# The normaliser of a gated linear-attention block: absolute value moved to ScalarE, EPS folded in once per group

## The reference, cut to what matters

```python
log_f = jax.nn.log_sigmoid(fg)
cs = jnp.cumsum(log_f, axis=1)
log_D = where(tril, cs[:, :, None] - cs[:, None, :], -inf) + ig[:, None, :]
max_log_D = jnp.max(log_D, axis=-1, keepdims=True)
D_mat = jnp.exp(log_D - max_log_D)
C = (qk / sqrt(DH)) * D_mat
normalizer = jnp.maximum(jnp.abs(C.sum(axis=-1, keepdims=True)), jnp.exp(-max_log_D))
h = jnp.einsum('hst,htd->hsd', C / (normalizer + EPS), vh)       # EPS = 1e-6
h = layernorm(h) * ln_scale
...
x = x + tanh(g_xattn) * h_all_heads
h = jnp.square(jax.nn.relu(layernorm(x) @ W_fc.T)); y = h @ W_proj.T
x = x + tanh(g_ffn) * mean(five spike steps of y)
```

## Time and profile before

| | |
|---|---|
| three runs | 617.12, 615.51 and 617.72 us, median 617.12 us |
| profiled execution, span from first to last instruction | 615.3 us; the page gives no other time for it |
| instructions | 17747 |
| busy: PE, DVE, ACT, POOL | 571.4, 526.3, 485.8, 493.3 us |
| share of the chain that ended last: PE | 82% |
| the same: queue of SP, DMA | 7%, 3% |

### The profile page before, as it was taken

How to read it: one execution, slowest core, us unless ns; L and a number is a source line. 1 busy time by engine, 2 the same in 40 slices (tenths; PEclk the granted TensorE clock), 3 DMA queues, 4 the chain that set the end, 5 groups by cost and what they waited for, 6 DMA issues and landing times.

```text
span 615.3 us, 17747 instructions
## 1 busy us (share of the span) xinstructions
PE 571.4 (93%) x6032; PEld 479.2 (78%) x6032; DVE 526.3 (86%) x1291; ACT 485.8 (79%) x1011; POOL 493.3 (80%) x541
## 2 busy tenths in 40 slices
PE   0568988999999999999999999999999999999995
PEld 0357888887888888888788888888888888887894
DVE  4789889989989898989989898989999888878446
ACT  3776878897888888888888788888888777776673
POOL 4878889996997889887997889887997887955542
PEclk9995989999999999999999999999999999999998
DMA  8775736664664637662663637752675427401002
GB/s 271 168 145 115 160 74 124 168 139 95 124 149 96 155 84 127 171 146 70 123 163 83 158 83 131 187 126 70 121 167 130 87 48 148 121 4 35 0 2 70
DMA packets 73193, 71.34 MB, mean 116 GB/s; under 512 B 8720, under 2 KB 68752, under 8 KB 73104
## 3 DMA queue, kind: packets, MB, share of 16 engines
q1 hardware_dynamic: 71888, 70.00, 50.5%
q10 hardware_dynamic: 1216, 0.21, 0.2%
HBM read 27.44 MB, written 8.39 MB: 58 GB/s over the span
## 4 chain that ended last, share of the span: by engine, by line
PE 82%; SPq 7%; DMA 3%; ACT 2%; issue 2%; DVE 2%; POOL 1%; ACTq 0%; POOLq 0%; DVEq 0%
PE z_ps L1069 28%; PE y_ps L1135 26%; PE qk_ps L773 4%; PE arg_ps L758 4%; PE misc_ps L503 4%; SPq L706 3%; PE misc_ps L569 2%; SPq L553 2%; PE pv_ps L822 2%; PE pv_ps L820 2%; PE pv_ps L821 2%; PE pv_ps L897 2%; DMA x<-w_proj_t 2%; PE y_ps L1164 1%; PE arg_ps L1135 1%
## 5 line engine op out<-in xcount | busy, mean ns | idle before, releaser
L802 POOL TENSOR_TENSOR c_lo<-decay 128x512 bf16<-128x512 f32 x128 | 132.7, 1043 | 31.9 <-DVE decay L792 31.8
L1112 POOL TENSOR_TENSOR sq_lo<-w_raw,sq_hi 128x512 fp32r<-128x512 f32 (+1 forms) x96 | 111.8, 1166 | 39.6 <-ACT w_raw L1092 39.3
L1069 PE MATMUL z_ps<-x_hi,wfc_hi 128*128 128x512 f32 (+1 forms) x288 | 114.4, 397 | 1.8 <-ACT w_raw L1079 1.8
L1069 PE MATMUL z_ps<-x_hi,wfc_lo 128*128 128x512 f32 (+1 forms) x288 | 106.1, 368 | 0.0
L1069 PE MATMUL z_ps<-x_lo,wfc_hi 128*128 128x512 f32 (+1 forms) x288 | 105.9, 368 | 0.0
L1135 PE MATMUL y_ps<-sq_hi,wpr_hi 128*128 128x512 f32 (+1 forms) x256 | 103.8, 406 | 0.0
L1135 PE MATMUL y_ps<-sq_hi,wpr_lo 128*128 128x512 f32 (+1 forms) x256 | 97.4, 380 | 0.0
L1135 PE MATMUL y_ps<-sq_lo,wpr_hi 128*128 128x512 f32 (+1 forms) x256 | 97.1, 379 | 0.0
L792 DVE TENSOR_TENSOR decay<-qk_ps,decay 128x512 f32<-128x512 f32 x128 | 87.0, 680 | 9.4 <-ACT decay L784 6.5
L784 ACT ACTIVATE decay<-arg_ps,lqk_col 128x512 f32<-128x512 f32 x128 | 86.6, 677 | 10.5 <-PE arg_ps L761 9.5
L1153 DVE SCALAR_TENSOR_TENSOR spikes<-y_ps,spikes 128x1024 bf16<-128x1024 f32 (+1 forms) x64 | 73.8, 1153 | 1.2
(11 more groups left out here) (193 smaller groups left out, 1727.8 us busy)
## 6 DMA issues: line engine op xcount, KB each, us to landing
x_in<-x SPq DMA_DIRECT2D x32, 256.0 KB, 3.2
kT_in<-ctx_cols SPq DMA_DIRECT2D x32, 256.0 KB, 3.2
v_in<-ctx_rows SPq DMA_DIRECT2D x32, 256.0 KB, 4.3
k_stack<-kT_hi SPq DMA_DIRECT2D x64, 128.0 KB, 3.2
k_stack<-kT_lo SPq DMA_DIRECT2D x64, 128.0 KB, 3.7
q_stack<-qT_hi SPq DMA_DIRECT2D x64, 128.0 KB, 4.1
q_stack<-qT_lo SPq DMA_DIRECT2D x64, 128.0 KB, 4.3
out<-w_raw SPq DMA_DIRECT2D x32, 256.0 KB, 3.4
```

The source lines that it names most:

```text
L802: e.tensor_tensor(c_lo[i % NCH][:, :], c, top(c), ALU.subtract).then_inc(sem("c_lo"), 1)
L1069: ins = e.matmul(z_ps[:, tokens(q)], lhsT, rhs, start=(n == 0), stop=(n == len(terms) - 1))
L1112: e.tensor_tensor(sq_lo[n % NSQ][:, tokens(q)], relu[n % NRE][:, tokens(q)], sq_hi[n % NSQ][:, tokens(q)].bitcast(fp32), ALU.subtract).the ...
```

## The change

`h_norm` is cut into six steps. On VectorE remain `h_scale` (the former L912), `h_add` (L913), `h_denom` (one scalar_tensor_tensor: add EPS, then max with the bound), `h_recip` (L918) and `h_norm` (L919); they stand next to each other at every place where `h_norm` stood. `h_abs` is new on ScalarE: Abs of the row sums, from PSUM to PSUM, once for each batch, 32 in all. `floor_eps` is new on GpSimd: it adds EPS to the bound, once for each of the ten groups, in place, ahead of `k_weigh` of the group's first batch. The tile `most` goes. Links within VectorE become semaphores of their own, waited for ahead of each step. The rest of the diff writes out loops that were there before (the order of the shared PSUM bank, and the programs' loops), with the same steps in the same order; TensorE's and SP's programs hold the same steps as before.

```diff
-        most = sb("most", [P, ST, NH], fp32)
...
+        def floor_eps(e, g):
+            if not 0 <= g < NG:
+                return
+            e.wait_ge(sem("fT_free"), g + 1)
+            least = floor[g % 3][:, 0:ST, 0:group_rows(g)]
+            e.tensor_scalar(least, least, EPS, None, ALU.add).then_inc(sem("floor_eps"), 1)
...
-            link(e, "vector", e.tensor_tensor(by_head(state_f[:, :]), inter_ps.rearrange("p c (g e) -> p c g e", g=HPC), since, ALU.mult))
-            link(e, "vector", e.tensor_tensor(pv_heads[:, 1, :, :], pv_heads[:, 1, :, :], late, ALU.add))
-            row_sum, least = pv_heads[:, :, :, DH], floor[g % 3][:, 0:ST, row:row + NH]
-            link(e, "vector", e.scalar_tensor_tensor(most[:, :, :], row_sum, -1.0, least, ALU.mult, ALU.max))
-            link(e, "vector", e.tensor_tensor(denom, row_sum, most[:, :, :], ALU.max))
-            link(e, "vector", e.tensor_scalar(denom, denom, EPS, None, ALU.add))
-            link(e, "vector", e.reciprocal(rdenom[:, :, :], denom))
+            e.tensor_tensor(by_head(state_f[:, :]), inter_ps.rearrange("p c (g e) -> p c g e", g=HPC), since,
+                            ALU.mult).then_inc(sem("h_scale"), 1)
+
+        def h_add(e, b):
+            e.wait_ge(sem("h_scale"), b + 1)
+            e.tensor_tensor(pv_heads[:, 1, :, :], pv_heads[:, 1, :, :], late, ALU.add).then_inc(sem("h_add"), 1)
+
+        def h_abs(e, b):
+            e.wait_ge(sem("h_add"), b + 1)
+            e.activation(denom, pv_heads[:, :, :, DH], ACT.Abs).then_inc(sem("h_abs"), 1)
+
+        def h_denom(e, b):
+            e.wait_ge(sem("h_abs"), b + 1)
+            if b == GROUPS[g][0]:
+                e.wait_ge(sem("floor_eps"), g + 1)
+            e.scalar_tensor_tensor(denom, denom, EPS, floor[g % 3][:, 0:ST, row:row + NH],
+                                   ALU.add, ALU.max).then_inc(sem("h_denom"), 1)
+
+        def h_recip(e, b):
+            e.wait_ge(sem("h_denom"), b + 1)
+            e.reciprocal(rdenom[:, :, :], denom).then_inc(sem("h_recip"), 1)
```

More of the change, by code:

```diff
@@ L206, in misc_order @@
         def misc_order():
[L208 to L218, removed]
+            return [("q", 0), ("g", 0), ("q", 1), ("gT", 0), ("q", 2), ("g", 1), ("fT", 0), ("gT", 1), ("q", 3),
[13 rows of a table added]
         MISC_ORDER = misc_order()
@@ L1769, in vector_program @@
             q_lo(e, 7)
+            h_scale(e, 2)
+            h_add(e, 2)
+            h_denom(e, 2)
+            h_recip(e, 2)
             h_norm(e, 2)
@@ new lines, in gpsimd_program @@
+            square_lo(e, 2, 4)
+            square_lo(e, 2, 5)
+            k_weigh_lo(e, 7)
+            square_lo(e, 2, 6)
+            square_lo(e, 2, 7)
+            c_lo_step(e, 7, 0)
+            am_split(e, 4, 1)
+            am_split(e, 4, 3)
+            state_lo(e, 7)
+            c_lo_step(e, 7, 1)
+            v_hi_step(e, 8)
+            square_lo(e, 3, 0)
+            c_lo_step(e, 7, 2)
+            square_lo(e, 3, 1)
+            c_lo_step(e, 7, 3)
+            floor_eps(e, 4)
+            k_weigh(e, 8)
@@ new lines, in gpsimd_program @@
+            c_lo_step(e, 11, 0)
+            am_split(e, 5, 1)
+            am_split(e, 5, 3)
+            state_lo(e, 11)
+            c_lo_step(e, 11, 1)
+            v_hi_step(e, 12)
+            square_lo(e, 5, 0)
+            c_lo_step(e, 11, 2)
+            square_lo(e, 5, 1)
+            c_lo_step(e, 11, 3)
+            floor_eps(e, 5)
+            k_weigh(e, 12)
+            v_lo_step(e, 12)
+            c_lo_step(e, 12, 0)
+            k_hi(e, 16)
+            square_lo(e, 5, 2)
+            k_weigh_lo(e, 12)
@@ new lines, in gpsimd_program @@
+            v_hi_step(e, 16)
+            square_lo(e, 7, 0)
+            c_lo_step(e, 15, 2)
+            square_lo(e, 7, 1)
+            c_lo_step(e, 15, 3)
+            floor_eps(e, 6)
+            k_weigh(e, 16)
+            v_lo_step(e, 16)
+            c_lo_step(e, 16, 0)
+            k_hi(e, 20)
+            square_lo(e, 7, 2)
+            k_weigh_lo(e, 16)
+            k_lo(e, 20)
+            c_lo_step(e, 16, 1)
+            square_lo(e, 7, 3)
+            c_lo_step(e, 16, 2)
+            c_lo_step(e, 16, 3)
@@ new lines, in gpsimd_program @@
+            c_lo_step(e, 19, 3)
+            floor_eps(e, 7)
+            k_weigh(e, 20)
+            v_lo_step(e, 20)
+            c_lo_step(e, 20, 0)
+            k_hi(e, 24)
+            square_lo(e, 9, 2)
+            k_weigh_lo(e, 20)
+            k_lo(e, 24)
+            c_lo_step(e, 20, 1)
+            square_lo(e, 9, 3)
+            c_lo_step(e, 20, 2)
+            c_lo_step(e, 20, 3)
+            state_lo(e, 20)
+            k_hi(e, 25)
+            k_weigh(e, 21)
+            square_lo(e, 9, 4)
@@ new lines, in gpsimd_program @@
+            k_weigh_lo(e, 23)
+            square_lo(e, 10, 6)
+            square_lo(e, 10, 7)
+            c_lo_step(e, 23, 0)
+            am_split(e, 8, 1)
+            am_split(e, 8, 3)
+            state_lo(e, 23)
+            c_lo_step(e, 23, 1)
+            v_hi_step(e, 24)
+            square_lo(e, 11, 0)
+            c_lo_step(e, 23, 2)
+            square_lo(e, 11, 1)
+            c_lo_step(e, 23, 3)
+            floor_eps(e, 8)
+            k_weigh(e, 24)
+            v_lo_step(e, 24)
```

950 lines of the change are left out of this document (607 added, 343 removed), and 13 rows, old and new, of the table SLOTS.

## The result

The changed kernel takes 621.76 us (median of 5 runs, 621.12 to 624.78), the kernel before in the same series 617.12 us (5 runs, 614.95 to 619.52). The ratio is 1.0085, 95% interval 1.0056 to 1.0114. It is slower, by 4.6 us; 618.0 us was forecast, and the measured time lies above the range.

A forecast was written before the change was run, and what follows sets the result against it. TensorE was taken to bound the repeated rounds, with VectorE or ScalarE steps mattering only in the first 160 us. 0.8 (beginning) + 0.1 (rounds) + 0 (GpSimd) = +0.9 us, 618.0 us on the median's scale; range 614.7 to 620.3.

The forecast's parts named there:

- 0 to 0.1 us a round on PE, so 0.1 us for all: Repeated rounds: delays from the Abs, about 1.1 us a round, mostly meet idle ScalarE time; 0.1 us in all reaches TensorE.
- I cost it at nothing: `floor_eps` on GpSimd, ten times ahead of `k_weigh`, 3.2 us in all: covered by 9.5 us idle per round, so 0.
- ScalarE's pushes, the main rival (0.12): Every round: the Abs delays Exp or `relu_step`, all 1.1 us reaches TensorE; 624.5 us, centre about 621; chance 0.12.
- the mark of 0.38 us a round: Extra time per round from which the rival of ScalarE delays reaching TensorE was to be decided (6 × 0.38 + 0.8 = 3.1 us).
- The chain itself: Each batch, L913's end to reciprocal: 0.56 us instead of 0.68, Abs at 0.20 us; gain 0.12 us where ScalarE is free.
- VectorE as a hidden bound (0.06): Rounds: TensorE's busy time hides waits for VectorE, so less VectorE work gives up to 8.6 us, 609.4 us; chance 0.06.
- the rival of 0.12: Beginning: moved idle time makes a half-clock stretch come or go, about 1.75 us per 3.5 us; 619.7 or 616.2; chance 0.12.
- The table load: Each of 32 Abs needs table loads there and back, some 2 us each, 64 us in all, 681 us; chance below 0.01.
- The beginning, +0.8 us forecast: First 160 us: the Abs delays ScalarE steps in batches 3 and 4, reaching TensorE through L792; +0.8 us, bounds −0.8 to +2.0.
- the prediction's own test: Between 91 and 160 us: TensorE's waits for L792 should rise from 2.2 to about 3 us; shrinking means the prediction is wrong.
- the forecast's sign, slower: Whole kernel: +0.9 us on the span, 0.15% more, within what a measurement can tell from no change.

The follow-up runs named there:

- EPS alone: Against the kernel before: EPS added to the bound on GpSimd once per group, absolute value left on VectorE, no Abs, `most` kept; 618.36 us, ratio 1.0017.

## Why the prediction was wrong

**The term that failed is "0 to 0.1 us a round on PE, so 0.1 us for all".** A round is 0.67 us longer, and from `state(7)` to `state(31)` it comes to 4.3 us. It has two parts, and neither is the one that the term weighed. That the tile `most` goes has no term in the sum at all, and GpSimd's instruction stands in it at nothing.

- *TensorE's cadence, some 3 us (0.5 us a round).* By the starts it is 0.6 us a round; between the changed kernel and the one with `most` kept, which differ in this alone, 0.4 to 0.6 us arrive (69.52, 69.61, 69.74 against 69.11, 69.13, 69.13), in six rounds 3 us. Taking the tile away isn't free: it shifts every later tile by 64 bytes against the weights. No step and no rival had it, and the rows could not warn of it, since the trace of before has one layout only. That the layout does it is shown by putting 64 bytes back (cadence and round return), by shifting tiles in the kernel before (cadence and round go), and by moving the weights and all behind them along (nothing changes). How the chip comes to it is open.
- *GpSimd, 0.15 to 0.2 us a round, some 1 us in all.* The prediction wrote "I cost it at nothing; without that cover it would be 0.3 us a group". It took 9.5 us of GpSimd's idle time per round as cover. But the idle time lies elsewhere: between `floor_eps` and the `square_lo` for chunk 3 of job 7 there is one wait of 0.16 us, against a delay of 0.57. The size was off as well: one input, 0.368 us, against 0.317 for two inputs of the nearest row, where I had expected less. Its number for the case without cover was nearer than the one it took.

**The sum of these** is 3 + 1 = 4 of 4.3 us in the repeated part; rounds of the changed kernel in its two executions go from 69.47 to 69.74, so the remainder isn't assigned. The PE starts of the three rounds from `state(11)` to `state(23)` give the same picture, after against before: behind matmuls of `z_step` and `y_step` 0.75 us a round more, behind the one ahead of that `y_step` 0.08 more, behind the last small matmul of `arg` 0.15 less, in all 0.68. So waits give back a part of what the cadence costs.

**ScalarE's pushes, the main rival (0.12): wrong, and the forecast right here.** The pushes can be measured in the kernel with the Abs and with neither of the other two effects (`most` kept, EPS on VectorE). Timeline of ACT, batch 16:

```profile
310.63 0.68 ACT L795 ACTIVATE decay<-arg_ps,lqk_col 128x512 f32<-128x512 f32 x1
311.33 0.60 ACT L1123 ACTIVATE w_raw<-z_ps 128x512 f32<-128x512 f32 x1
```

Counted from `state(15)`, the Exp starts at 26.36 us, before at 25.81: 0.55 us late, forecast 0.60 to 0.70. The `relu_step` behind it starts at 27.06, before at 27.08: the wait of 0.62 us has taken the push up. At batches 15, 17 and 18 the pushes are 0.22, 0.04 and 0 us, in all 0.8 where the forecast had 1.1. The round is 68.93 us, before 68.94, so nothing of them reaches TensorE. The rival named the mark of 0.38 us a round, and 0.67 is over it; the mark was met by another mechanism. Had I stopped at the page and the windows, I would have taken this rival for proven.

**The chain itself.** The Abs took 0.168 us instead of 0.20, and the upper end of 0.29 did not come up. From the state's addition to the reciprocal it was 0.45 us in batch 16, forecast 0.56. The Trainium skill (ScalarE: Activation LUTs, "Rules for kernel authors") gives relu, max, min, add and mul to VectorE, for the rate per element; it doesn't name Abs there. The trace agrees in so far as nothing was won: 9.7 us of VectorE's work against 10.0 us of its waits, 0.31 for each. On 16 columns no cost shows either: ScalarE did it for 0.17 us, and with the layout kept and EPS off GpSimd TensorE's round stayed as it was. VectorE's busy time fell by 9.7 us instead of 11, ScalarE's rose by 4.3 instead of 6.4.

**VectorE as a hidden bound (0.06)**: no. With the cadence of before, the round with 0.36 us less work a batch is not shorter.

**The clock.** It changed as the rival of 0.12 has it, but to the good, a stretch of 3.4 us less. The second execution of the changed kernel has that stretch again (84.68 to 88.09 us), and the kernel before has one more in its second execution, so it comes and goes between executions of one program and is not shown to be an effect of the change. **The table load**: the changed kernel's trace has the same two loads at its beginning (2.4 and 5.1 us) and no other.

**The beginning, +0.8 us forecast: not decided.** From the first transposition to `state(7)` it is 130.1 us before and 131.6 after. But executions of five kernels with the order of before spread over 129.1 to 131.1 us (134.5 in the one with two stretches at half clock behind 80 us), and those of six with the changed order over 129.7 to 133.0. The means, 130.1 and 131.3, differ in the forecast's direction, with clocks that differ as well. PE's waits for the product of scores and decay between 91 and 160 us went from 2.2 us in four to 1.8 in three, where I had expected 3:

```profile
PE qk_ps L783 <- DVE decay L802: 1.8, 3, 0.8
```

By the prediction's own test this is against it. Neither a gain nor a loss is shown, so the forecast's sign, slower, came out right without its reason: the loss that was measured is in the rounds.

## What to carry to other kernels

A tile taken away, added or resized moves all that is allocated behind it. So before an edit's time is put down to its instructions, run it once with the old allocation kept (a tile that nobody uses), and run the old kernel once with the new one. When TensorE is busy throughout, don't look at its busy share but at the distance between the same instruction in two rounds, and at the starts of matmuls that follow each other without a wait. Idle time of an engine covers a new instruction only if it lies between that instruction and the next one that somebody is waiting for.

## What the runs showed of the hardware

- In seven of the kernels (the change with `most` kept, EPS alone, EPS on VectorE, the change with 64 bytes ahead of `x2_hi` or with the weights moved, and before with 128 bytes taken away or 32 added) VectorE waits 0.2 to 1.0 us, at one place near 426 us, for a DMA of x that isn't waited for in the others. Kernel with `most` kept, timeline of DVE:

```profile
426.59 0.75 DVE L399 BATCH_NORM_STATS2 stat<-x_in 128x6 f32<-128x256 f32 x2 [1.01 <-DMA x_in<-x]
```

  The round around it is 70.21 us instead of 69.13, so such a wait comes through whole. It can be a part of what is left of these kernels' ratios over 1, also of those of before with 128 bytes taken away and with 32 added, whose round there is 70.13 and 69.65 us. How often it comes in executions without a profile isn't known, and what delays the DMA is open.
